# Running the experts of a transformer layer only on the tokens that chose them, by an on-chip sort and indirect DMA

## The reference

```python
tok = h2.reshape(T, D)                          # 2048 tokens, D = 256
probs = softmax(tok @ gate_w.T)                 # E = 8 experts
topv, topi = top_k(probs, 2)
combine = zeros((T, E)); combine[t, topi] = topv / (sum(topv) + 1e-9)
eg, eu = tok @ wg[e].T, tok @ wu[e].T           # for every expert: I = 176
eo = (silu(eg) * eu) @ wd[e].T
hidden + sum_e combine[t, e] * eo[e, t]         # then x is added
```

## Time and profile before

| | |
|---|---|
| median of 3 runs | 1299.55 us |
| span of the profiled execution, first to last instruction | 1300.3 us |
| TensorE clock granted over the span | 0.987 of full |
| PE busy | 95% |
| DVE, ACT, POOL busy | 62%, 50%, 32% |
| DMA queues together | some 10% of 16 engines |

### The profile page before, as it was taken

The page is one execution under the profiler, slowest core; times in us unless marked ns, Lnnn a source line. Parts: engine busy times, 40 slices in busy tenths (PEclk is TensorE's granted clock), DMA queues, the critical chain, the costliest instruction groups (busy, mean ns, idle before and its releaser), DMA issues. The chain is left out here.

```text
span 1300.3 us, 23464 instructions
## 1 busy us (share of the span) xinstructions
PE 1241.6 (95%) x8088; PEld 1110.2 (85%) x8120; DVE 805.6 (62%) x1569; ACT 653.8 (50%) x1780; POOL 422.3 (32%) x499
## 2 busy tenths in 40 slices
PE   6999999999999999899979999999999998999998
PEld 5888999989998999788868888888898886788887
DVE  3666454335433543476668888888878876865554
ACT  3455444444444444545547676676667665333232
POOL 4111311131113111423376666666666660000000
PEclk9999999999999999999989999999999998999999
DMA  9100000000000020220110000000000021413210
GB/s 338 42 1 2 17 1 17 1 2 1 17 1 2 1 82 1 97 98 16 33 45 2 2 1 2 2 1 0 0 0 0 0 89 53 114 56 98 97 51 21
DMA packets 25166, 45.58 MB, mean 35 GB/s; under 512 B 3008, under 2 KB 15680, under 8 KB 24064
## 3 DMA queue, kind: packets, MB, share of 16 engines
q1 hardware_dynamic: 25024, 44.44, 10.1%
q10 hardware_dynamic: 64, 0.07, 0.0%
HBM read 42.30 MB, written 2.20 MB: 34 GB/s over the span
## 5 line engine op out<-in xcount | busy, mean ns | idle before, releaser
L493 POOL TENSOR_TENSOR p<-p,rinv 128x512 f32<-128x512 f32 x64 | 66.7, 1041 | 415.8 <-DVE rinv L1032 415.6
L762 ACT ACTIVATE p<-bank,nb,rq 128x128 f32<-128x128 f32 x256 | 113.8, 454 | 115.0 <-DVE nb L1240 115.0
L620 ACT ACTIVATE p<-bank,nmax 128x128 f32<-128x128 f32 x256 | 90.5, 366 | 119.6 <-DVE nmax L1020 119.6
L546 POOL TENSOR_TENSOR qr<-qr,rb 128x512 f32<-128x512 f32 x64 | 81.9, 1280 | 102.5 <-DVE rb L1206 102.1
L1429 PE MATMUL bank<-cur_hi,wqk_hi 128*128 128x512 f32 x256 | 110.1, 430 | 3.5 <-DVE cur_lo L973 3.5
L1028 DVE COPY pt<-bank 128x512 f32<-128x512 f32 x64 | 44.2, 690 | 110.6 <-PE bank L1447 107.8
L1429 PE MATMUL bank<-cur_hi,wqk_lo 128*128 128x512 f32 x256 | 102.9, 402 | 0.0
L1429 PE MATMUL bank<-cur_lo,wqk_hi 128*128 128x512 f32 x256 | 102.6, 401 | 0.0
L629 ACT ACTIVATE o_hi<-bank,bqkv 128x512 fp32r<-128x512 f32 x64 | 44.1, 688 | 101.1 <-PE bank L1457 101.1
L1036 DVE SCALAR_TENSOR_TENSOR o_lo<-bank,bqkv,o_hi 128x512 fp32r<-128x512 f32 x64 | 48.0, 750 | 51.8 <-ACT o_hi L629 51.8
L1688 PE MATMUL bank<-wo_hi,o_hi 128*128 128x256 f32 x256 | 74.4, 291 | 4.1 <-DVE o_lo L1279 4.1
(11 more groups left out here) (210 smaller groups left out, 4048.1 us busy)
## 6 DMA issues: line engine op xcount, KB each, us to landing
wqk_raw<-in_wqk SPq DMA_DIRECT2D x8, 512.0 KB, 9.9
gate<-gates_scratch SPq DMA_DIRECT2D x8, 512.0 KB, 3.7
cw<-combination_scratch SPq DMA_DIRECT2D x16, 256.0 KB, 3.2
xres<-in_x SPq DMA_DIRECT2D x4, 512.0 KB, 9.3
wv_raw<-in_wv SPq DMA_DIRECT2D x8, 256.0 KB, 9.9
wo_raw<-in_wo SPq DMA_DIRECT2D x8, 256.0 KB, 10.0
w_raw<-in_w SPq DMA_DIRECT2D x2, 1024.0 KB, 5.8
wq_raw<-in_wq SPq DMA_DIRECT2D x1, 2048.0 KB, 9.4
```

The source lines that it names most:

```text
L493: nc.gpsimd.tensor_tensor(p1[:, h % 2], p1[:, h % 2], rinv[:, h % 2].unsqueeze(2).broadcast_to([P, GB, T]), ALU.mult).then_inc(a_pn, 1)
L546: nc.gpsimd.tensor_tensor(qr[:, s.u % 2], qr[:, s.u % 2], rb[:], ALU.add).then_inc(g_qr, 1)
L620: last = nc.scalar.activation(p1[:, h % 2, b], bank[3][:, b * T:(b + 1) * T], ACT.Exp, bias=nmax[:, h % 2, b:b + 1], accum_out=rsum[:, h % ...
L762: last = nc.scalar.activation(p2[:, (s.u - 3) % 2, j], bank[3][:, j * T:(j + 1) * T], ACT.Exp, scale=rq[:, (s.u - 3) % 4, j:j + 1], bias=n ...
```

## The change

The tokens are dealt with in two chunks, 12 sequences and 4. For a chunk, `ranks` on PE and `dispatch` on DVE count, for each token and expert chosen, its place in a list sorted by expert, with each expert's part rounded up to whole tiles of 128 rows. POOL writes each token's normalised row to its two places in a DRAM scratch, by indirect DMAs of 128 rows (`send`: two for each sequence). The experts then run on 31 tiles for chunk 0 and 15 for chunk 1 (`TC`, always that many, 5888 rows in all): SP loads a tile, PE turns it, reads the tile's expert from a table into a register, and multiplies by that expert's weights; the result goes through ACT to a second DRAM scratch. When a chunk's tiles are stored, POOL fetches each sequence's two rows by indirect DMA (`fetch`), and DVE adds them, weighted, to the residual. The input is added on POOL beforehand. SP stores each sequence by itself.

The combination weights are no longer turned, stored and spread (`combination_transposes`, `combination_out`, `load_weights` are gone), nor are there `e_hi`, `e_lo`, `em`. The parts 1 to 3 of the routing of groups 0 to 2 move into steps 14 and 15 of groups 1 to 3 of the attention; POOL copies the normalised rows there (step 12). No expert product stands in the attention's tail. SP fills the token scratch with zeros during group 0 (6 MB written). `load_tile(0)` and `load_tile(31)` wait until all sends of their chunk have landed. The norm, routing, ranks and dispatch of group 3 stand among the tiles 1 to 15 on PE and DVE. The core of the diff:

```diff
+IC = I // 2
+BA = 12
+BC = (BA, B - BA)
+TC = tuple((n * T * 2 - 1) // P + E for n in BC)
+NT = sum(TC)
@@ sync
+            for i in range(NX - 1):
+                load_tile(i)
             sp.wait_ge(g_op, NG * 4 * GB)
+            load_input(0)
+            for i in range(NT):
+                if i + NX - 1 < NT:
+                    load_tile(i + NX - 1)
+                if i >= 4:
+                    store_tile(i - 4)
+                if i in (12, 16, 20):
+                    load_input((i - 8) // 4)
...
+            for b in range(B):
+                sp.wait_ge(m_y, 2 * b + 2)
+                sp.dma_start(out[b], xres[:, b]).then_inc(d_out, 16)
@@ gpsimd
+                if s.u == 12 and not s.first:
+                    pool.wait_ge(t_lp, s.g)
+                    for k in range(KD):
+                        last = nc.gpsimd.tensor_copy(span(act_t, k, s.g - 1), xn[:, 2 * k:2 * k + 2]...)
+            def send(c, b):
...
+                for k in range(2):
+                    nc.gpsimd.indirect_dma_start(
+                        out=xs_dram[c], out_offset=bass.IndirectOffsetOnAxis(ap=index[:, k, at:at + 1], axis=0),
+                        in_=row(g, at % GB), in_offset=None).then_inc(d_send[c], 16)
...
             attention2(pool, step)
+            for b in range(BC[0]):
+                send(0, b)
             norm(4 * NG - 1, True)
+            for g in range(NG):
+                add_input(g)
+            for b in range(BC[1]):
+                send(1, b)
+            stored(TC[0] - 1)
+            for b in range(BA):
+                fetch(b)
+            stored(NT - 1)
+            for b in range(BA, B):
+                fetch(b)
@@ scalar
+            for i in range(NT + 3):
+                if i < NT:
+                    x_hi(i)
+                if 0 <= i - 1 < NT:
+                    gate_silu(i - 1)
+                if 0 <= i - 2 < NT:
+                    h_hi3(i - 2)
+                if 0 <= i - 3 < NT:
+                    expert_out(i - 3)
@@ vector
+                if s.u == 14 and not s.first:
+                    routing_part(s.g - 1, 1)
+                if s.u == 15 and not s.first:
+                    routing_part(s.g - 1, 2)
+                    routing_part(s.g - 1, 3)
                 if s.u == 16:
-                    routing_part(0, 1)
+                    dispatch(0, 0)
                 if s.u == 17:
-                    routing_part(0, 2)
-                    routing_part(0, 3)
+                    dispatch(0, 1)
+                if s.u == 18:
+                    dispatch(0, 2)
...
+            FETCHED = TC[0] + 8
+            for i in range(NT + 3):
+                if i < NT:
+                    x_lo(i)
+                if 0 <= i - 1 < NT:
+                    hidden(i - 1)
+                if 0 <= i - 2 < NT:
+                    h_lo3(i - 2)
...
+                if i >= FETCHED:
+                    result(i - FETCHED)
@@ tensor
+            def gate_up(i):
...
+                e = pe.value_load(tile_e[0:1, i:i + 1], min_val=0, max_val=E - 1)
+                pe.wait_ge(e_xl, i + 1)
...
+                for k in range(KD):
+                    hi, lo = (w[k][:, bass.ds(e, 1), :].rearrange("p a n -> p (a n)") for w in (w3_hi, w3_lo))
+                    for j, (l, r) in enumerate(split_products(xt_hi..., xt_lo..., hi, lo)):
+                        last = pe.matmul(bank[1 + i % 2][:, 0:2 * I], l, r, ...)
+            for i in range(NT + 3):
+                if i < NT:
+                    tile_turned(i)
+                if 0 <= i - 1 < NT:
+                    expert[i - 1] = gate_up(i - 1)
+                if 0 <= i - 2 < NT:
+                    hidden_turned(i - 2)
+                if 0 <= i - 3 < NT:
+                    expert_down(i - 3, expert.pop(i - 3))
...
```

More of the change, by code:

```diff
@@ L183, in program @@
[L183 to L194, removed]
+        probs = sb("probs", [P, GB, E], at=W2 + 47 * KB)
@@ new lines, in program @@
+        two = sb("two", [P, 2, BA], at=W + 31 * KB + 384)
+        index = sb("index", [P, 2, B], U32, at=W + 31 * KB + 480)
+        weight = sb("weight", [P, 2, B], at=W + 31 * KB + 608)
+        tile_f = sb("tile_f", [P, 32], at=W + 31 * KB + 736)
+        tile_e = sb("tile_e", [P, NT], I32, at=W + 27 * KB + 768)
+        above = sb("above", [P, E, BA], at=place["gt"][0])
+        prefix = sb("prefix", [P, E, E], at=place["eq"][0])
+        match = sb("match", [P, 2, BA, E], at=place["gt"][0])
@@ L301, in attention2 @@
                 step(Step(NG - 1, u, False))
[L303 to L310, removed]
[L312 removed]
+        W3_STEP = 5
         def late_chunk(u):
             c = u - (4 * GB + 1)
[L317 removed]
+            return None if not 0 <= c < 6 else (c // 3, c % 3, slice(3 * (c % 3), min(3 * (c % 3) + 3, E)))
         def pair_part(c, i):
@@ L893, in norm_apply_rms, with norm_rows, rows_turned @@
                 last.then_inc(n_xn, 1)
+            def norm_rows(n, g):
+                dve.wait_ge(n_rs, n + 1)
+                dve.wait_ge(d_router, 32)
+                for b in range(GB):
+                    last = nc.vector.scalar_tensor_tensor(
+                        out=xn[:, b], in0=xres[:, bass.ds(g * GB + b, 1), :].rearrange("p a d -> p (a d)"),
+                        scalar=rstd[:, b:b + 1], in1=w_row[:], op0=ALU.mult, op1=ALU.mult)
+                last.then_inc(n_xn, 1)
+            def rows_turned(n, g, k, src):
+                dve.wait_ge(n_tp, 2 * n + k + 1)
+                nc.vector.tensor_copy(span(act_t, k, g), src[:]).then_inc(n_ev, 1)
             def norm_weight(n, g, k, kind, src):
@@ L1392, in _ @@
+            for b in range(NT + 3 - FETCHED, B):
+                result(b)
         @block.tensor
@@ new lines, in _ @@
+            expert = {}
+            for i in range(NT + 3):
[7 more added lines that the diff above has]
+                    expert_down(i - 3, expert.pop(i - 3))
+                if i == 4:
+                    pe.wait_ge(g_qt, NG * 4 * GB)
+                    pe.wait_ge(g_pl, NG * 4 * GB)
+                    pe.wait_ge(n_xn, 4 * NG)
+                    for k in range(KD):
+                        norm_transposes(4 * NG - 1, k, bank[4 + k])
+                if i == 6:
+                    router_product(NG - 1, bank[4])
+                if i == 7:
+                    pe.wait_ge(t_lt, NG)
+                    router_transposes(NG - 1, bank[4])
+                if i == 12:
+                    ranks(1)
```

689 lines of the change are left out of this document (386 added, 303 removed).

## The result

The changed kernel takes 1284.53 us, the median of 4 runs (1278.81 to 1288.42), against 1301.01 us (1298.91 to 1302.59) for the kernel before beside it: ratio 0.9871, 95% interval 0.9843 to 0.9899.

A forecast was written before the change was run, and what follows sets the result against it. The prediction took PE to bound the kernel (busy 95%) and 88 us of its work to go. The last product at 1256.3 plus 20.5 us of end gave 1277 us against 1300.3; range 1255 to 1295, 8 in 10 within 1243 to 1322.

The forecast's parts named there:

- POOL free for the sends: End of attention: POOL's last `p2` ends at 1089.7 before, plus 4.5, minus 1.7, so sends can start at 1092.5.
- first tile to the end of the last product: Expert tiles: 112.7 us for 46 tiles, plus clock, fill and drain, group 3's work and DVE bursts; from 1129.4 to 1256.3.
- the attention drift, +4.5 us: Attention groups 1 to 3: routing in steps 14 and 15 and small additions cost about 1.5 us a group, mostly absorbed by slack.
- the tail's own -1.7: Attention's tail on DVE: group 0's routing and `cur_lo` go, 14 small dispatch operations (3.2 us) come; net -1.7 us.
- One indirect DMA: Sends and fetches on POOL: one of 128 rows takes 1.3 us, sized from POOL's 512-column work of 1.04 to 1.28.
- Rival 1: POOL's queue becomes the bound: at 1.82 us or more per indirect DMA the end passes 1300; chance 0.17.
- rival 3: Tiles and POOL's DMAs both flow: 2.12 us a tile, 0.87 us an indirect DMA, 1248 us in all; chance 0.20.
- One tile: Tile loop on PE: 2.12 us of work plus 0.33 us for the register load, 2.45 us a tile.
- Rival 2: PE's stream doesn't flow in the tiles: at 2.96 us a tile the end passes 1300; chance 0.07.
- 3 + 3.2 + 3: Among the tiles, in us: 3 until the clock is back, 3.2 for group 3's PE work, 3 for DVE bursts.
- Rival 4: DVE's work stretches POOL's DMAs: each fetch among the tiles takes 2.5 us, end at 1308; chance 0.04.
- Hidden fetches: Chunk 0's 24 fetches on POOL, 31.2 us, run from 1221.4 to 1252.6 under chunk 1's tiles.

The follow-up runs named there:

- e1: The kernel before, with only routing parts 1 to 3 of groups 0 to 2 moved into steps 14 and 15 of the next group's attention; 1309.40 us, ratio 1.0042.
- e9: The changed kernel with 16 extra DVE additions (six of 128 x 1536, ten of 128 x 512) behind its last split; single execution, 1319.98 us.
- e5: The changed kernel with each tile's expert a constant in place of the register loaded from SBUF; 1278.86 us.
- the second execution: The changed kernel as it is, run once more beside the other experiments; 1287.90 us, ratio 0.9895.
- e6: The changed kernel with the final additions three tiles later (from iteration 42, not 39) and 12 extra DVE operations beside the sends; 1281.93 us.
- e2: The changed kernel with routing parts 1, 2 and 3 in steps 13, 14 and 15, each ahead of DVE's wait for the exponentials; 1279.59 us, ratio 0.9816.

## Why the prediction was right, and which term was not

The forecast was 1277.0 us, with 1243 to 1322 around it; 1284.53 was measured, 7.5 us above the forecast and on the side that had 0.66. The picture of the stages was right: what the tiles save, and that the queue of sends and the fetches at the end eat most of it. That the number came so near is partly luck, as the table shows. Against the profiled span, 1286.7, the terms come out like this:

| step of the prediction | predicted | measured | difference |
|---|---|---|---|
| POOL free for the sends | 1092.5 | 1105.1 | +12.6 |
| 24 sends | 31.2 | 32.8 | +1.6 |
| landing and load of tile 0 | 5.7 | 3.7 | -2.0 |
| first tile to the end of the last product | 126.9 | 124.6 | -2.3 |
| the end | 20.5 | 20.5 | 0 |

*The term that was mis-sized* is "the attention drift, +4.5 us". I subtracted DVE's idle share of a step, 5.5 - 4.24 us, from the work put there. That idle time isn't slack at the place where the work went: it is DVE waiting for ACT inside a chain that DVE started, and work put behind these waits and in front of `cur_lo` lengthens the chain by its whole length, and by the PE wait and the clock it brings. The forecast had the last `p2` 2.8 us later (4.5 - 1.7); it is 15.4 later. Of these, groups 1 and 2 are longer by 5.6 and 5.5 us, step 14 of the third by 1.3 and the tail behind it by 2.2; 0.5 stand ahead of group 1. How the 2.2 split into parts 2 and 3 of the third group and the tail's own -1.7 was not measured. With 3.8 for these parts (the lengthening of step 15 in e1) the -1.7 comes out near -1.6, and the drift at 16.2 in place of 4.5; that is an estimate. e1 gave 5.1 of the 5.6 with nothing else changed.

*One indirect DMA*, 1.3 us, was right: 1.26 us, or 1.37 with what DVE's splits stretch. The reason given, POOL's 512-column work as the nearest row, holds as a size only: e9 shows that a send has a wait for DVE in it that no row of arithmetic had shown. Rival 1 needed 1.82 and is refuted; rival 3's 0.87 wasn't reached either.

*One tile*, 2.45 us, was too much: PE's work was counted right, 2.12 us (e5 measured 2.12), and the register load costs about 0.1 where I took 0.33 from the earlier trace rows. Rival 2 is refuted. The gain from it, 46 x 0.24 = 11 us, is mostly used up in the sum: the first 15 tiles took 46.2 us, 3.08 each (44.7 in the second execution), which is 13 over their steady pace where I had 3 + 3.2 + 3, and the stop at iteration 39 took 3.5 to 4.6. Which part of the 13 is clock, and which group 3's norm, routing and dispatch, isn't separated here. The Trainium skill (DMA: Bandwidth & Descriptors, latency and other measured facts) gives some 600 ns as the floor of such a load. The trace doesn't agree: the 46 loads have a median of 307 ns, and only the longest reach 592. Their time was mostly hidden, as my lower bound had it.

*DVE and POOL.* I had said that nothing stretches POOL's arithmetic and that a DMA's case was open. e9 and the 57 long sends show a send held until the DVE operation beside it ends. The Trainium skill (SBUF — State Buffer, the box on DVE blocking DMA) says that GpSimd is locked out while such an operation runs, and the traces agree; I set it aside on rows of arithmetic. The box speaks of a mode that copies use; here additions with two SBUF operands held sends too. How long a send takes depends on the operation beside it: 1.15 or 1.49 us in e9's trains, 1.07 to 2.83 beside the splits (1.67 to 1.81 in the changed kernel), against the 3.1 us for every DMA that my sum tried. Rival 4's 2.5 us a fetch wasn't seen: fetches beside DVE's additions lasted at most 1.28 us (1.42 in the second execution).

*Hidden fetches* were right, but only just: I had chunk 0's end at 1252.6, 3.7 us before the last product's end; it came at 1265.4, 0.8 before. POOL then still waits 5.67 us for the last tiles to be stored, so nothing was lost. I had named the wait at iteration 39 as a danger of "about 2 us in my sum"; it was 1.86 us at DVE, and e6 shows that it costs PE 3.5 to 4.6.

So the number was near for two reasons. The largest new term, the queue of sends, was taken from the right neighbour. And, by luck, the 12.6 us that were missing in front of the sends stood beside two overestimates of 2.0 and 2.3, and the second is itself what is left of 11 us too much for the pace of the tiles and some 8 too little for their start and the stop.

## What to carry to other kernels

An engine's idle share in a pipelined loop doesn't tell its slack: ask whether the idle time is a wait for something that this engine itself set off. New work in front of an operation that others wait for (here `cur_lo`) costs its length and what the waiting engine then loses; ahead of the wait it cost less (e2). Behind `cur_lo` it might cost less still, which no run tried. A serial queue of indirect DMAs that stands between two stages should start while its engine still waits in the stage before; six of 24 moved up gave 7.7 us, all that they take. And a consumer that waits in the common stream for a distant transfer costs more than its wait: put it a few iterations later.

## What the runs showed of the hardware

- An indirect DMA of 128 rows of 1 KB takes POOL 0.96 us (scatter) or 0.95 (gather) and 0.30 us to the next.
- It waits for the end of a DVE operation beside it that reads SBUF alone, and ends 0.83 to 0.85 us (scatter) behind that end, in all 57 stretched sends of twelve traces: 1.79 us apart beside additions of 1.76 us, 1.45 beside operations every 0.725 us.
- The reverse was in e2: DVE operations of 0.17 and 0.42 us lasted 0.94 and 1.38 us, and ended 0.03 and 0.29 us behind POOL's sum of two SBUF operands.
- The granted clock was 0.50 in the first 5 us of tiles whether PE had idled 26, 6.7 or 4.2 us.
- Loading an expert number from SBUF into a PE register takes 0.31 us (median of 46; 0.30 to 0.59) and the address work 0.15, and the two cost a tile about 0.1 us (2.12 us without, 2.21 and 2.25 with).
- After the same PE wait of 2.3 us in the same code, the granted clock of the next 4 us was 0.58 in one execution and 1.00 in another, which is worth 1.5 us.
